# Expert layers on all tokens inside the edge loop, and a row carry patched by one gather and one scatter

## What is computed

```python
h = (t @ W_gat).reshape(M, 4, 4)                 # t: normalised tokens, M = 16384
e = leaky_relu(a_src[src] + a_dst[dst])          # 524288 edges; those with dst >= M fall away
ee = exp(e - segment_max(e, dst)[dst])
agg = segment_sum(h[src] * (ee / denom[dst]), dst) + b_gat
scores = layernorm(agg).reshape(M, 4, 4).mean(1)
w = softmax of the two best scores of a token
for ei in range(4):
    g = w where expert ei is one of the two, else 0
    hh = gelu(t @ W1[ei] + b1[ei])               # 128 -> 256
    out = out + g * (hh @ W2[ei] + b2[ei])       # 256 -> 128
x = x + out
```

## Time and profile before

| | us |
|---|---|
| median of 3 runs | 8349.21 (8320.61 to 8353.12) |
| the profiled execution, its time | 8372.14 |
| its span, first to last instruction | 8370.3 |
| busy in the span: PE, DVE, ACT, POOL | 3157.4, 3508.5, 1356.3, 2734.2 |
| largest share of the chain that ended last | POOL, line 869, 26% |

### The profile page before, as it was taken

The page is one execution under the profiler, slowest core; times in us unless marked ns, Lnnn a source line. Parts: engine busy times, 40 slices in busy tenths (PEclk is TensorE's granted clock), DMA queues, the critical chain, the costliest instruction groups (busy, mean ns, idle before and its releaser), DMA issues.

```text
span 8370.3 us, 87470 instructions
## 1 busy us (share of the span) xinstructions
PE 3157.4 (38%) x33420; PEld 2006.3 (24%) x33421; DVE 3508.5 (42%) x7512; ACT 1356.3 (16%) x3665; POOL 2734.2 (33%) x2630
## 2 busy tenths in 40 slices
PE   0011148766875977468750000000000000001999
PEld 0011037425632762256220000000000000001555
DVE  9999737556655755356541111111111111103222
ACT  0000036205510731055100000000000000000222
POOL 0000230001000000220007777777777777673000
PEclk9955579858875986588755555555555555555999
DMA  2000130010001000200021111111111111111111
GB/s 69 0 0 0 51 111 3 1 22 22 2 1 32 3 2 0 34 3 2 0 29 13 21 16 21 16 16 21 17 16 21 17 16 21 19 10 13 38 38 36
DMA packets 239761, 162.30 MB, mean 19 GB/s; under 512 B 115566, under 2 KB 209147, under 8 KB 238524
## 3 DMA queue, kind: packets, MB, share of 16 engines
q0 software_dynamic: 85536, 39.23, 6.2%
q1 hardware_dynamic: 82572, 66.35, 2.7%
q10 hardware_dynamic: 71312, 51.92, 2.5%
HBM read 68.42 MB, written 87.83 MB: 19 GB/s over the span
## 4 chain that ended last, share of the span: by engine, by line
PE 31%; POOL 29%; DVE 16%; issue 13%; DVEq 6%; ACT 2%; DMA 1%; another core or an unknown queue 1%; POOLq 0%; ACTq 0%; SPq 0%
POOL SA_ L869 26%; PE PSB L1070 3%; PE PSB L614 3%; DVE SA_ L1201 3%; PE PSB L1064 3%; PE PSB L630 2%; PE PSB L354 2%; DVE SA_ L1191 2%; PE PSB L494 2%; PE PSB L1068 2%; POOL SB_ L878 1%; POOL VPAD L875 1%; PE PSB L324 1%; PE PSB L364 1%; ACT PRX L277 1%
## 5 line engine op out<-in xcount | busy, mean ns | idle before, releaser
L869 POOL DMA_INDIRECT SA_<-s_T,GIX x2048 | 2180.2, 1065 | 662.3 <-issue 662.3
L943 PE MATMUL PSB<-LCD,IDW 128*128 128x1 f32 x2 | 0.6, 348 | 2952.5 <-DVEq L843 2952.5
L861 POOL DMA_INDIRECT s_AEXP<-fill,SIX x128 | 129.4, 1011 | 2350.1 <-DMA fill<-s_ADT 2309.0
L824 DVE TENSOR_TENSOR XPAD<-SA_ 128x256 f32<-128x256 f32 x32 | 13.9, 435 | 2040.4 <-DMA SA_<-s_T,GIX 2040.4
L943 PEld LDWEIGHTS PSB<-LCD,IDW 128*128 128x128 f32 x2 | 0.5, 312 | 2952.6 <-issue 2952.6
L783 POOL DMA_INDIRECT SA_<-s_SK,BLKI x128 | 121.2, 947 | 1021.9 <-DVE BLKI L1334 980.3
L851 ACT ACTIVATE SB_<-SB_ 128x512 f32<-128x512 f32 x32 | 20.1, 629 | 2589.0 <-DVE SB_ L831 1830.0
L277 ACT ACTIVATE PRX<-PSB,MX 128x144 f32<-128x144 f32 x1024 | 375.3, 380 | 209.8 <-DVE MX L203 209.7
L1305 PE MATMUL PSB<-ident,SA_ 128*128 128x128 f32 x448 | 84.3, 372 | 837.9 <-DVE SA_ L1272 576.1
L1097 DVE SCALAR_TENSOR_TENSOR XPAD<-PSB,G,XPAD 128x128 f32<-128x128 f32 x512 | 179.7, 351 | 486.3 <-PE PSB L1070 421.5
L1064 PE MATMUL PSB<-XPAD,SA_ 128*128 128x512 f32 x512 | 226.9, 596 | 394.1 <-DMA XPAD<-s_X 394.1
(11 more groups left out here) (349 smaller groups left out, 8132.1 us busy)
## 6 DMA issues: line engine op xcount, KB each, us to landing
SA_<-s_T,GIX POOLq DMA_INDIRECT x2048
...
s_X<-SA_ ACTq DMA_DIRECT2D x4, 2048.0 KB, 8.7
s_TNT<-XPAD ACTq DMA_DIRECT2D x4, 2048.0 KB, 6.2
...
```

The source lines that it names most:

```text
L869: pool.indirect_dma_start(out=n.G[:,s,c,:],out_offset=None,in_=d["T"],in_offset=IOA(ap=n.GIX[s][:,c:c+1],axis=0)).then_inc(n.gath[s],16)
```

## The change

Four things are done.

- **Experts.** The function `moe_*` is split in two. `experts_act` and `experts_pe` compute the outputs of all four experts for all tokens, without the gates, and write them to a new tensor `Y` in memory (2048 values for each partition and chunk of 512 tokens, 1 MB a chunk, 32 MB in all; a partition's row of `Y` is 512 KB long). They stand inside the edge loop: iteration `i` does its edges if `i < V`, and then two chunks of tokens if `i < 16`. ScalarE itself issues the loads of `TNT` and the stores of `Y`, and copies each output from PSUM to one buffer `YB`. TensorE runs the 16 turns ahead of the carry.
- **Mix.** After the gates, `mix_sync` loads `Y` (1 MB) and the tokens (256 KB) of a chunk into one of four buffers, `mix_dve` does 16 multiply-adds from SBUF, four for each expert with a drain between experts, and ScalarE stores the chunk.
- **Carry.** Only the last edge of the first destination of a row can need what is passed on. `edges_prep_dve` finds its place (`FEI`) with a scan, a multiply-add and a minimum over 4095 columns. After the edge loop POOL waits for all of `Y` and for the cleared part of `R`, gathers one row of `R` a partition, VectorE merges it with the carried values, POOL scatters it back and waits for that. Then come the 128 gathers of line 875; the 128 gathers of line 878, the table `CT` and what `node_dve` did with it are gone.
- **Weights.** The experts' weights are loaded by SP ahead of the second load of `ADN`, into tiles that the attention used.

Cut to its core:

```diff
 def edges_prep_dve(dve,n,SA,V,ones,K,row):
...
+    one=ones[:,0:1].to_broadcast((P,COLS-1))
+    dve.tensor_tensor_scan(d[:,1:],one,one,0.0,ALU.mult,ALU.add); dve.drain()
+    dve.scalar_tensor_tensor(out=d[:,1:],in0=k[:,1:],scalar=BIG,in1=d[:,1:],op0=ALU.mult,op1=ALU.add); dve.drain()
+    dve.tensor_reduce(n.FEF[:,0:1],d[:,1:],AX.X,ALU.min); dve.drain()
+    dve.tensor_scalar(n.FEF[:,0:1],n.FEF[:,0:1],K[:,0:1],-1.0,ALU.min,ALU.add); dve.drain()
+    dve.scalar_tensor_tensor(out=n.FEI[:,:],in0=row,scalar=float(COLS),in1=n.FEF[:,0:1],op0=ALU.mult,op1=ALU.add).then_inc(n.fe_rdy,1)
...
 def edges_act(act,n,PSB,d,V):
...
+    act.wait_ge(n.fe_rdy,1); act.wait_ge(n.moe_w,64)
     with act.Fori(0,NCH//2) as i:
         with act.If(i<V): chunks(i)
+        with act.If(i<NCK//2): experts_act(act,n,PSB,d,i)
...
 def edges_pool(pool,n,d,tick,V):
...
     for s in range(2): pool.wait_ge(n.rst[s],V*16+1); pool.sem_inc(tick,1)
-    pool.wait_ge(n.r_fill,BLOCKS*96)
+    pool.wait_ge(n.y_st,16*NCK+1); pool.wait_ge(n.r_fill,BLOCKS*96); pool.wait_ge(n.fe_rdy,1)
+    pool.indirect_dma_start(out=n.FE[:,:],out_offset=None,in_=d["R"],in_offset=IOA(ap=n.FEI[:,:],axis=0)).then_inc(n.fe_g,16)
+    pool.wait_ge(n.fo_rdy,1)
+    pool.indirect_dma_start(out=d["R"],out_offset=IOA(ap=n.FEI[:,:],axis=0),in_=n.FO[:,:],in_offset=None).then_inc(n.fo_st,16)
+    pool.wait_ge(n.fo_st,16)
     for t in range(NT):
         pool.indirect_dma_start(out=n.RE[:,t,:],out_offset=None,in_=d["R"],in_offset=IOA(ap=n.EIX[:,t:t+1],axis=0)).then_inc(n.re_g,16)
-    pool.wait_ge(n.lc_st,16)
-    for t in range(NT):
-        pool.indirect_dma_start(out=n.CE[:,t,:],out_offset=None,in_=d["CT"],in_offset=IOA(ap=n.PIX[:,t:t+1],axis=0)).then_inc(n.ce_g,16)
...
 def edges_sync(sp,n,d,SA,tick,V):
...
     sp.wait_ge(n.bar_dve,SE*IMGS)
+    for dst,k in ((n.WM1,"W1"),(n.WM2,"W2"),(n.B1M,"b1mT"),(n.B2M,"b2m")):
...
+        sp.dma_start(dst,src).then_inc(n.moe_w,16)
     sp.dma_start(n.ADN[:,first:],adt[:,first:]).then_inc(n.ad_ld2,16)
...
+def experts_act(act,n,PSB,d,i):
+    for s in range(2):
+        act.wait_ge(n.moe_ys,i*8+1)
+        act.dma_start(n.TNC[:,s,:],d["TNT"][:,bass.ds(i*1024+512*s,512)]).then_inc(n.moe_in,16)
+    for s in range(2):
+        j=i*2+s
+        for m in range(8):
+            act.wait_ge(n.moe_h,j*8+(m+1))
+            if m==0: act.wait_ge(n.moe_ys,j*4+1)
+            act.activation(n.HM2[:,m,:],PSB[:,(m%4)*512:(m%4+1)*512],ACT.Gelu,bias=n.B1M[:,m:m+1]).then_inc(n.moe_ge,1)
+        act.wait_ge(n.y_st,j*16+1)
+        for t in range(4):
+            act.wait_ge(n.moe_ys,j*4+(t+2))
+            act.activation(n.YB[:,512*t:512*t+512],PSB[:,(4+t)*512:(5+t)*512],ACT.Copy).then_inc(n.moe_ev,1)
+        act.drain()
+        act.dma_start(d["Y"][:,bass.ds(j*2048,2048)],n.YB).then_inc(n.y_st,16)
+def mix_sync(sp,n,d,tick):
+    sp.wait_ge(n.edges_done,1); sp.wait_ge(n.y_st,16*NCK+1)
...
+            sp.dma_start(n.YC[s],d["Y"][:,bass.ds(j*2048,2048)].rearrange("p (t c) -> p t c",t=4)).then_inc(n.mix_in[s],16)
+            sp.dma_start(n.X3C[s],x3[:,bass.ds(j*4,4),:]).then_inc(n.mix_in[s],16)
...
+def mix_dve(dve,n):
+    with dve.Fori(0,NCK//MIX) as i:
+        for s in range(MIX):
+            j=i*MIX+s
+            dve.wait_ge(n.mix_in[s],i*32+32)
+            for e in range(4):
+                for t in range(4):
+                    x=n.X3C[s][:,t,:]
+                    last=dve.scalar_tensor_tensor(out=x,in0=n.YC[s][:,t,e*P:(e+1)*P],scalar=n.G4[:,bass.ds(j*4+t,1),e],in1=x,op0=ALU.mult,op1=ALU.add)
+                if e<3: dve.drain()
+            last.then_inc(n.mix_dv,1)
...
-            carry_pe(pe,n,PSB,ident)
-            moe_pe(pe,n,PSB,ones)
+            experts_pe(pe,n,PSB,ones)
+            carry_pe(pe,n,PSB,ident)
```

More of the change, by code:

```diff
@@ L787, in pos_pool, with edges_prep_dve @@
         pool.indirect_dma_start(out=I[:,t*128:(t+1)*128],out_offset=None,in_=rows,in_offset=IOA(ap=m.QI[:,t:t+1],axis=0)).then_inc(n.a2_ld,16)
-def edges_prep_dve(dve,n,SA,V):
+def edges_prep_dve(dve,n,SA,V,ones,K,row):
     I=SA.bitcast(i32)
@@ L921, in carry_dve @@
     dve.tensor_tensor(n.LCD[:,3:4],n.LCD[:,0:1],PSB[:,0:1],ALU.is_equal); dve.drain()
+    dve.tensor_scalar(n.FEF[:,1:2],n.LCD[:,3:4],-1.0,BIG,ALU.add,ALU.mult)
     dve.tensor_tensor(n.LCD[:,2:3],n.LCD[:,2:3],n.LCD[:,3:4],ALU.mult); dve.drain()
@@ L1034, in node_act, with experts_pe @@
     act.activation(SA[:,t1:t1+NT],SA[:,t1:t1+NT],ACT.Exp).then_inc(n.nd3e,1)
-NCK=NODES//512
-def moe_sync(sp,n,d,tick):
-    sp.wait_ge(n.edges_done,1)
-    for dst,k in ((n.WM1,"W1"),(n.WM2,"W2"),(n.B1M,"b1mT"),(n.B2M,"b2m")):
-        src=d[k]
-        if k=="W1": src=src.rearrange("e c h -> c e h")
-        if k=="W2": src=src.rearrange("e (f p) o -> p (e f) o",p=P)
-        if k=="b2m": src=src.rearrange("e c -> (e c)").rearrange("(a n) -> a n",a=1)
-        sp.dma_start(dst,src).then_inc(n.moe_w,16)
-    x3=d["X3"].rearrange("(t p) c -> p t c",p=P)
-    sp.wait_ge(n.g_rdy,1)
-    def load(i):
+def experts_act(act,n,PSB,d,i):
[14 more added lines that the diff above has]
+        act.dma_start(d["Y"][:,bass.ds(j*2048,2048)],n.YB).then_inc(n.y_st,16)
+def experts_pe(pe,n,PSB,ones):
+    pe.wait_ge(n.moe_w,64)
+    with pe.Fori(0,NCK//2) as i:
+        pe.wait_ge(n.moe_in,i*32+32)
         for s in range(2):
             j=i*2+s
-            if not (isinstance(i,int) and i==0): sp.wait_ge(n.moe_out[s],i*16); sp.sem_inc(tick,1)
-            sp.dma_start(n.TNC[:,s,:],d["TNT"][:,bass.ds(j*512,512)]).then_inc(n.moe_in[s],16)
-            sp.dma_start(n.X3C[:,s],x3[:,bass.ds(j*4,4),:]).then_inc(n.moe_in[s],16)
-    load(0)
-    with sp.Fori(1,NCK//2) as i: load(i)
-def moe_pe(pe,n,PSB,ones):
-    pe.wait_ge(n.moe_w,64)
-    with pe.Fori(0,NCK//2) as i:
-        for s in range(2):
-            j=i*2+s
-            pe.wait_ge(n.moe_in[s],i*32+32)
             for m in range(8):
@@ L1081, in moe_pool @@
-def moe_pool(pool,n,out,tick):
-    o=out.rearrange("(t p) c -> p t c",p=P)
-    with pool.Fori(0,NCK//2) as i:
-        for s in range(2):
-            j=i*2+s
-            pool.wait_ge(n.moe_dv,j*4+5); pool.sem_inc(tick,1)
-            pool.dma_start(o[:,bass.ds(j*4,4),:],n.X3C[:,s]).then_inc(n.moe_out[s],16)
-    for s in range(2): pool.wait_ge(n.moe_out[s],NCK//2*16)
-def moe_dve(dve,n,PSB):
-    with dve.Fori(0,NCK//2) as i:
-        for s in range(2):
-            j=i*2+s
-            for t in range(4):
-                dve.wait_ge(n.moe_ys[s],i*4+(t+2))
-                for e in range(4):
-                    x=n.X3C[:,s,t,:]
-                    last=dve.scalar_tensor_tensor(out=x,in0=PSB[:,(4+t)*512+e*P:(4+t)*512+(e+1)*P],scalar=n.G4[:,bass.ds(j*4+t,1),e],in1=x,op0=ALU.mult,op1=ALU.add)
-                    if e<3: dve.drain()
-                last.then_inc(n.moe_dv,1)
+                    last=pe.matmul(PSB[:,(4+t)*512+(m//2)*P:(4+t)*512+(m//2+1)*P],n.HM2[:,m,P*t:P*(t+1)],n.WM2[:,m,:],start=False,stop=(m==7),skip_group_check=True)
@@ new lines, in experts_pe, with load @@
+                last.then_inc(n.moe_ys,1)
+def mix_sync(sp,n,d,tick):
+    sp.wait_ge(n.edges_done,1); sp.wait_ge(n.y_st,16*NCK+1)
+    x3=d["X3"].rearrange("(t p) c -> p t c",p=P)
+    def load(i):
+        for s in range(MIX):
+            j=i*MIX+s
+            if not (isinstance(i,int) and i==0): sp.wait_ge(n.mix_out[s],i*16); sp.sem_inc(tick,1)
+            sp.dma_start(n.YC[s],d["Y"][:,bass.ds(j*2048,2048)].rearrange("p (t c) -> p t c",t=4)).then_inc(n.mix_in[s],16)
+            sp.dma_start(n.X3C[s],x3[:,bass.ds(j*4,4),:]).then_inc(n.mix_in[s],16)
+    load(0)
+    with sp.Fori(1,NCK//MIX) as i: load(i)
@@ new lines, in mix_dve, with mix_act @@
+def mix_dve(dve,n):
+    with dve.Fori(0,NCK//MIX) as i:
+        for s in range(MIX):
+            j=i*MIX+s
+            dve.wait_ge(n.mix_in[s],i*32+32)
[5 more added lines that the diff above has]
+            last.then_inc(n.mix_dv,1)
+def mix_act(act,n,out,tick):
+    o=out.rearrange("(t p) c -> p t c",p=P)
+    with act.Fori(0,NCK//MIX) as i:
+        for s in range(MIX):
+            act.wait_ge(n.mix_dv,i*MIX+(s+1)); act.sem_inc(tick,1)
+            act.dma_start(o[:,bass.ds((i*MIX+s)*4,4),:],n.X3C[s]).then_inc(n.mix_out[s],16)
+    for s in range(MIX): act.wait_ge(n.mix_out[s],NCK//MIX*16)
@@ L1401, in _ @@
             for b in range(BEFORE,IMGS): image(b)
[L1402 removed]
+            edges_prep_dve(dve,n,m.SA,V,ones,m.KV[:,1,:],m.PF[:,0:1])
             edges_dve(dve,n,m.SA,V)
@@ L1405, in _ @@
             node_dve(dve,n,m.SA)
-            moe_dve(dve,n,PSB)
+            mix_dve(dve,n)
         @block.scalar
         def _(act):
-            for q in n.moe_ys: act.sem_inc(q,1)
+            act.sem_inc(n.y_st,1)
             sort_act(act,m,PSB)
```

131 lines of the change are left out of this document (65 added, 66 removed).

## The result

The changed kernel takes 8224.86 us (median of 4 runs, 8204.73 to 8247.15) where the kernel before, run beside it, takes 8346.81 us (4 runs, 8320.61 to 8353.12). The ratio is 0.9868 (95% interval 0.9836 to 0.9899): 1.3% faster. The forecast was 7790 us in 7700 to 7920: the sign is right, the gain is 122 us where 557 were forecast. The profiled execution took 8238.87 us, its span 8237.0.

A forecast was written before the change was run, and what follows sets the result against it. POOL's issue of the 2048 edge gathers sets the pace, with the experts behind them on an otherwise idle PE. Terms -671 + 178 - 115 - 7 + 48 + 10 = -557 gave 7790 us, range 7700 to 7920.

The forecast's parts named there:

- Their new place costs nothing as long as ScalarE is back in time: Edge loop: the experts, moved beside the edge gathers, leave the end for minus 671 us at no cost there.
- about 47 us: Edge loop: length of an experts' turn of two chunks, 2 x 21 us plus 3 us for the first load.
- 130 us: Edge loop: a turn of experts could last up to about this long before POOL waited.
- Rival D: Edge loop: ScalarE becomes the bound; past 130 us a turn, each us costs 16 and one more at the end; chance 0.02.
- Company of the gathers, +48: Edge gathers: stores and loads beside them cost 1.5 us a chunk, 48 us in all, bounds 0 and 96.
- rival C: Edge gathers and mix: everything hidden, gathers keep 1.388 us, mix 163 us, result 7720 us; chance 0.15.
- The seam: Between edge gathers and gathers of `R`: uncovered last turn, then 9 us of fetch, merge and scatter; plus 54 us.
- Mix, +178: Final stage replacing the experts: 5.4 us a chunk for 32 chunks and 5 for the ends; bounds 163 and 266.
- Preparation, +10: Edge preparation: scatters held beside two more VectorE operations, 3.3 us each, and about 3 for weight loads; bounds 0 and 16.
- Nodes and `CT`: After the edge loop: node work minus 7 us; gathers of `CT` gone, net minus 115 with the later `R` gathers.

The follow-up runs named there:

- the first comparison: The changed kernel against the kernel before, chip not on record: 8224.86 us beside 8346.81 us, ratio 0.9868.
- chip 15: One of the three chips of the follow-up runs (14, 15 and 1), on each of which the kernel before takes 7812 to 7823 us.
- e5: Kernel before plus 256 independent 128x128 float32 products on PE between last image and carry, on three chips: 7832.09, 7812.97 and 7802.56 us.
- e8: Changed kernel with every Gelu of the experts done five more times: 7287.53 us.
- e9: Changed kernel with twelve more Gelus for each of the experts' Gelus: 8317.87 us.
- a1: Changed kernel, no edit, on another chip: 7217.92 us beside 7821.99 us of the kernel before, ratio 0.9226.

## Why the prediction was wrong

Each interval by POOL's first and last instruction or VectorE's first, in us: the first comparison, then chip 15, where the trace of the probe kernel e5 stands for the kernel before. Each row is rounded by itself.

| | forecast | first: before | after | change | chip 15: before | after | change |
|---|---|---|---|---|---|---|---|
| edge preparation | +10 | 54.8 | 67.6 | +13 | 54.8 | 67.7 | +13 |
| edge gathers | +48 | 2841.1 | 3303.2 | **+462** | 2610.0 | 2609.3 | -1 |
| last edge gather to first of `R` | +54 | 33.2 | 137.9 | **+105** | 17.3 | 83.3 | +66 |
| gathers of `R` (and `CT`) | -169 | 333.7 | 163.8 | -170 | 328.9 | 163.9 | -165 |
| nodes | -7 | 68 | 60 | -8 | 68 | 60 | -8 |
| experts, or mix | -493 | 670 | 164 | -506 | 680 | 164 | -516 |
| all ahead of it (images, sort) | 0 | | | -29 | | | +25 |
| sum | -557 | | | -133 | | | -585 |

The row on the images is scatter: that point lies between 4044 and 4116 us in the fourteen traces of those chips, whichever kernel it is.

**The step that failed** is "Their new place costs nothing as long as ScalarE is back in time", with its "about 47 us" a turn. The condition was right and so was its bound (130 us; e8 and e9 put it at about 144). The 47 us were taken from the earlier trace rows, rows of the experts' stage at the end, in which POOL issues 32 plain stores, and carried into a stage in which it issues 2048 gathers. In the first comparison the turn is 192 us there. On chip 15 it is 50 us and the mechanism holds: the medians of a1 give a gain of 604 us, where 557 were forecast. A duration taken from a stage with another neighbour was not a row for this place, and the trace had rows for engines beside POOL's transfers: operations of VectorE 1.40 us apart, 86 products of PE in 187 us. At 1.40 us each, the 352 instructions of a turn would be 493 us, far past the bound.

**Rival D** named the wait and what releases it, and had 0.02, with the same 47 us as the argument against it. It should have had the chance that those rows left open. Its price was also off: by its formula a turn of 192 us gives 7880 + 17 x 62 = 8934 us, measured 8225. The gathers between the pauses ran at 1.268 us and not 1.388 (2048 x 0.12 is 246 us). There were 14 pauses of 50 us, 706 us, and not 16 of 62, 992 us, since the turn may last some 140 and not 130. And the last turn, with no gathers beside it, took 56 us (7772.79 to 7828.36) and not 192.

**The other steps.** *Company of the gathers, +48:* nothing to see on chip 15 (-1), rival C's value. There one gather in 64 starts 2.4 us after the one before it, with the new stores and without. The forecast's base of 1.388 us a gather was itself of the first setting: on chip 15 the kernel before has 1.274 (2610/2048). Why it fell to 1.268 with the change in the first comparison no run shows. *The seam:* on chip 15 the last turn took 6767.83 to 6821.45, 53.6 us, as worked out (53); fetch to first gather of `R` 16 us instead of 9. In the first comparison the seam grew by 105: the last turn began 62 us after the last edge gather and not 24, since the turn before it had still to end. *Mix, +178:* 164 us. It is VectorE's pace, 16 multiply-adds and drains in 5.13 us a chunk, the bound from below. The Trainium skill's 207 GB/s for rows 512 KiB apart (DMA: Bandwidth & Descriptors, Latency and other measured facts) made the mix an estimated 248 us. The page's figure is of copies from memory to memory, and the mix took 164 us here: the last stretch of the table above moved 275 GB/s in all, the stores of `Y`, with the same row pitch, landed 3.9 us after their issue for 1 MB (269 GB/s), and VectorE waited for a transfer once, for 1.0 us. The loads of `Y` alone were not put to the test, since VectorE set their pace. *Preparation, +10:* +13, for the reason given: about 3 for the weight loads, and 10 in place of 7 for scatters held beside VectorE. VectorE's scan and the scatter beside it, of the first trace after the change:

```profile
4352.11 8.69 DVE L814 TENSOR_TENSOR_SCAN SA_<-ones 128x4095 f32<-128x4095 f32 x1
```
```profile
4352.32 9.25 POOL L873 DMA_INDIRECT s_AEXP<-fill,SIX  x1 [0.30 <-issue]
```

The scatter ends with the scan again, as in the earlier trace rows; the scan is twice as long as the comparison there (8.69 against 4.42 us). *Nodes and `CT`* came out within 4 us. On chip 15 rival C (all hidden, 629 us below) was nearer than the forecast (25 us off, against 47), and its values for the gathers and the mix are the measured ones.

**What stays open.** That instructions came slowly beside POOL's indirect transfers in the first comparison is shown by PE's rows in the edge loop and VectorE's in image 1, both 1.40 us apart. That a turn of some 200 us makes such pauses is shown by e9. That the slow instructions made the turn long is argued: the copies' 50 us fit 36 instructions at 1.40 us, but by PE's rows the products ended 62 to 88 us before the copies that wait for them. Whether the number of PE's instructions is what costs there (theory I), and what is different in that setting, could not be tried: all three chips of the experiments had the other pace. Two causes are ruled out by rows. It is no traffic of data: the slow stretch moves 9 GB/s, the fast one on chip 15 35 GB/s. And it is no refill of instructions. The Trainium skill (Runtime: NRT & Kernel Launch, Instruction fetch mechanics) says that an engine's instructions come in blocks of 16 KiB through a DMA queue of its own. The profile of the first trace agrees in size ("q8 instruction: 244, 4.00", 16 KB each), but between 4900 and 7700 us of it no packet of an instruction queue is listed (three and two in the slow stretches of the images):

```profile
q0 software_dynamic: 54522, 17.56, 12.2%
q10 hardware_dynamic: 11232, 54.53, 5.1%
q1 hardware_dynamic: 7344, 4.23, 0.5%
```
